# A two-layer graph kernel in float32: x kept on chip, a fourth PSUM bank for second products, and 110 adjacency tiles loaded in pairs

## The reference

```python
# x, u: 8192 x 64;  adj: 8192 x 8192;  weight: 64 x 64;  bias: 64;  all float32
x1 = layernorm(x + adj @ (x * (u >= 0.1) / 0.9))
x2 = layernorm(x1 + adj @ (x1 @ weight) + bias)
```

## Time and profile before

| | |
|---|---|
| median of 3 runs | 898.15 us (898.11 to 898.16) |
| profiled execution | 898.45 us, span 896.5 us, granted clock 0.995 |
| PE busy | 863.1 us, 96% |
| DVE busy | 560.9 us, 63% |
| read from memory | 356.61 MB |
| transfers of 1 MB | 334 |

### The profile page before, as it was taken

One profiled execution on the slowest core, in us unless ns is written; L12 is line 12 of the kernel. 1 busy time (PEld: TensorE's weight loads), 2 busy tenths in 40 slices (PEclk: granted clock), 3 DMA queues, 4 the chain that ended last, 5 costly groups with the idle time before them and its releaser, 6 DMA issues.

```text
span 896.5 us, 15757 instructions
## 1 busy us (share of the span) xinstructions
PE 863.1 (96%) x6790; PEld 482.7 (54%) x6790; DVE 560.9 (63%) x1144; ACT 21.3 (2%) x59; POOL 25.3 (3%) x24
## 2 busy tenths in 40 slices
PE   3899999999999999999999999999999999999996
PEld 2664554445767546555555564646545566456432
DVE  6356123145155757775777777778777777867755
ACT  0100000000000000000000000000000000000011
POOL 3000000000000000000000000000000000000133
PEclk9999999999999999999999999999999999999998
DMA  9999999999999999999999999999999999999962
GB/s 373 412 416 420 421 419 420 421 420 421 420 420 420 419 421 419 421 400 402 420 421 406 423 419 397 419 372 422 372 410 421 415 423 419 420 423 419 420 256 71
DMA packets 55412, 359.73 MB, mean 401 GB/s; under 512 B 6448, under 2 KB 10544, under 8 KB 12592
## 3 DMA queue, kind: packets, MB, share of 16 engines
q1 hardware_dynamic: 55344, 358.74, 96.9%
HBM read 356.61 MB, written 2.10 MB: 400 GB/s over the span
## 4 chain that ended last, share of the span: by engine, by line
PE 85%; DMA 7%; DVE 4%; SPq 2%; issue 2%; ACT 0%; POOLq 0%; POOL 0%; DVEq 0%
PE psum L1033 20%; PE psum L986 19%; PE psum L967 8%; PE psum L1001 8%; PE psum L995 8%; PE psum L1019 6%; DMA tiles<-adj_chunks 5%; PE psum L953 5%; PE psum L974 4%; PE psum L1039 4%; DMA tiles<-adj_t 2%; PE psum L930 1%; SPq L500 1%; DVE layer L654 1%; DVE layer L709 1%
## 5 line engine op out<-in xcount | busy, mean ns | idle before, releaser
L986 PE MATMUL psum<-tiles,stat 128*64 128x256 f32 x1952 | 218.3, 379 | 1.6 <-DMA tiles<-adj_t 1.6
L1033 PE MATMUL psum<-tiles,stat 128*64 128x512 f32 x944 | 210.3, 593 | 0.6 <-issue 0.3
L654 DVE TENSOR_TENSOR layer<-psum,layer 128x512 f32<-128x512 f32 (+1 forms) x143 | 98.7, 690 | 154.6 <-PE psum L1033 58.0
L986 PEld LDWEIGHTS psum<-tiles,stat 128*64 128x64 f32 x1952 | 147.1, 137 | 72.4 <-issue 7.5
L1033 PEld LDWEIGHTS psum<-tiles,stat 128*64 128x64 f32 x944 | 69.2, 137 | 119.8 <-issue 115.8
L690 DVE TENSOR_TENSOR tiles<-tiles 128x512 f32<-128x512 f32 x90 | 62.2, 691 | 53.8 <-PE psum L976 52.2
L1003 PE MATMUL psum<-tiles,stat 128*64 128x256 f32 x360 | 92.6, 380 | 0.0
L969 PE MATMUL psum<-tiles,stat 128*64 128x256 f32 x360 | 92.4, 379 | 0.0
L967 PE MATMUL psum<-tiles,stat 128*64 128x256 f32 x360 | 92.4, 379 | 0.0
L967 PEld LDWEIGHTS psum<-tiles,stat 128*64 128x64 f32 x360 | 49.3, 137 | 37.8 <-issue 16.7
L678 DVE TENSOR_TENSOR tiles<-tiles 128x512 f32<-128x512 f32 x90 | 60.6, 684 | 8.0 <-DMA tiles<-adj_t 8.0
(11 more groups left out here) (100 smaller groups left out, 852.5 us busy)
## 6 DMA issues: line engine op xcount, KB each, us to landing
tiles<-adj_t SPq DMA_DIRECT2D x306, 1024.0 KB, 13.6
tiles<-adj SPq DMA_DIRECT2D x12, 1024.0 KB, 19.2
tiles<-adj_chunks SPq DMA_DIRECT2D x12, 1024.0 KB, 20.4
tiles<-xu SPq DMA_DIRECT2D x4, 1024.0 KB, 8.0
tiles<-adj_parts SPq DMA_DIRECT2D x16, 256.0 KB, 17.6
x_res<-x SPq DMA_DIRECT2D x16, 128.0 KB, 14.4
out<-layer SPq DMA_DIRECT2D x8, 256.0 KB, 2.2
w<-weight SPq DMA_DIRECT2D x4, 16.0 KB, 10.2
```

What stands on the lines that cost most here:

```text
L654: return dve.tensor_tensor(out=to, in0=addend, in1=to, op=ALU.add)
L986: last = pe.matmul(sum_f[i % 2][to, left], stat[:, j * C + c, 0:D], tile[:, c, columns], start=begun.get("f") != i and c == 0, stop=ends a ...
L1033: last = pe.matmul(bank[to, :], stat[:, j * C + c, D:2 * D], tile[:, c], start=c == 0, stop=c == C - 1)
```

## The change

1. **x kept.** ACT copies x out of the staged `xu` into `stat[:, :, D:2D]` at the start (four copies of 128 x 1024), the place where h will stand later. The 16 loads of `x_res` and their waits on SP go. Loads into the last four slots wait for these copies too.
2. **Fourth bank.** `turned` moves to columns 256 to 511 of the two `sum_f` banks, whose sums fill columns 0 to 255, and `ECHO_BANKS` becomes 4. The rows that next use such a bank wait for `turned_read`, where they waited for the copy of the sum. The old use of 3 in `order_of_work` becomes `JOINS_LAST` = 2, so that the last `chunk` and `rest` of column 0 stand one job earlier in row 2.
3. **Pairs.** Tiles that are on chip for fewer than `SHORT` = 4 jobs are loaded two by two where a slot with an even number and its neighbour are both free no later than `LATER` = 1 job after the second-earliest free slot. The host lays such tiles side by side (`adj_twos`), so that a partition's row is 16 KB long, and one transfer of 2 MB brings both and adds to one semaphore. 110 tiles in 55 transfers are loaded so. Single tiles take, of the free slots, the one whose neighbour is busy longest. All counts `freed` are kept in rising order.

```diff
-ECHO_BANKS = 3
+ECHO_BANKS = 4
+JOINS_LAST = 2
+SHORT = 4
+LATER = 1
+TWOS_OF = ("early", "pair", "first", "raw")
...
-            if pieces and (len(filler) == ECHO_BANKS if i > 1 else len(filler) % 2 == 0):
+            if pieces and (len(filler) == JOINS_LAST if i > 1 else len(filler) % 2 == 0):
...
+    def short(n):
+        tile, begin, uses = needs[n]
+        return len(tile) == 2 and uses[-1] - begin < SHORT and tile_jobs[begin][0] != "part"
...
+    n = 0
+    while n < len(needs):
+        in_order = sorted(free)
+        if n + 1 < len(needs) and short(n) and short(n + 1) and (
+                tile_jobs[needs[n][1]][0] in TWOS_OF):
+            freed, slot = min((max(free[s], free[s + 1]), s) for s in range(0, SLOTS - 1, 2))
+            if freed <= min(needs[n][1], max(latest, in_order[1]) + LATER):
+                take(n, slot)
+                take(n + 1, slot + 1)
+                latest = max(latest, freed)
+                freed_of[n] = freed_of[n + 1] = latest
+                beside[n] = n + 1
+                n += 2
+                continue
+        ready = max(latest, in_order[0])
+        slot = -max((latest > 0 and free[s ^ 1] if s ^ 1 < SLOTS else latest, -free[s], -s) for s in range(SLOTS) if free[s] <= ready)[2]
+        latest = freed_of[n] = ready
+        take(n, slot)
+        n += 1
...
-        x_res = sb("x_res", [P, 2, C * D])
...
-        h_bias = [x_res[:, :, :].rearrange("p n (c d) -> p (n c) d", d=D),
-                  halves[:, :].rearrange("p (c d) -> p c d", d=D)]
+        h_bias = [layer1[:, n].rearrange("p (c d) -> p c d", d=D) for n in (1, 2)]
...
-        turned = banks[4]
-        echo = banks[5:8]
+        turned = [bank[:, B // 2:B] for bank in sum_f]
+        echo = banks[4:8]
...
-                if rows_begun == 0 and part == 1 or rows_begun >= 1 and kind in ("first", "fused") and tile[0] == rows_begun:
-                    i = rows_begun
-                    if i >= 2:
-                        sp.wait_ge(turned_read, turns(i - 2))
-                    sp.dma_start(x_res[:, i % 2], x_v[:, i]).then_inc(s_res[i % 2], 16)
-                    rows_begun += 1
-                if new and staged <= slot:
+                tile, both = loaded[0], len(loaded) == 2
+                if new and staged <= slot + both:
                     sp.wait_ge(dropped, XU)
+                    sp.wait_ge(x_kept, XU)
                 if freed:
                     sp.wait_ge(tile_jobs_done, freed)
+                if both:
+                    sp.dma_start(tiles[:, slot:slot + 2], adj_twos[n_twos]).then_inc(s_arrived[slot], 16)
+                    n_twos += 1
+                    continue
...
+            for g in range(XU):
+                act.wait_ge(s_xu[g], 16)
+                act.activation(rows_of_x(g, slice(D, 2 * D)), xu_stage[:, g, :, 0], ACT.Copy).then_inc(x_kept, 1)
...
-                x_rows = x_res[:, i % 2].rearrange("p (c d) -> p c d", c=C)
+                x_rows = stat[:, i * C:(i + 1) * C, D:2 * D]
...
-                            if i <= 2:
-                                pe.wait_ge(half_by_act, turns(i - 2))
-                            pe.wait_ge(half_by_dve, turns(i - 2))
+                            pe.wait_ge(turned_read, turns(i - 2))
```

More of the change, by code:

```diff
@@ L268, in place_tiles, with take @@
                 del on_chip[tile]
[L270 to L277, removed]
+    def short(n):
+        tile, begin, uses = needs[n]
+        return len(tile) == 2 and uses[-1] - begin < SHORT and tile_jobs[begin][0] != "part"
+    free, latest = [0] * SLOTS, 0
+    slot_of, freed_of, beside = {}, {}, {}
+    def take(n, slot):
+        tile, begin, uses = needs[n]
+        assert free[slot] <= begin, "the order of work needs more slots"
+        free[slot] = uses[-1] + 1
         for m in uses:
             slot_of[m, tile] = (slot, n)
+    n = 0
[17 more added lines that the diff above has]
+        n += 1
     loads, place, landed, whole = [], {}, [0] * SLOTS, set()
+    signal, used = {}, set()
     for m, job in enumerate(tile_jobs):
@@ L288, in place_tiles, with tiles_side_by_side, resnorm_graph_layers @@
                 first_load = n not in whole
+                new = slot not in used
+                tiles_loaded = [tile]
                 whole.add(n)
-                loads.append((tile, job[1] if in_parts else None, slot, freed_of[n] if first_load else 0,
-                              landed[slot] == 0, job[0]))
                 landed[slot] += first_load
-            place[job, tile] = (slot, landed[slot])
+                signal[n] = slot, landed[slot]
+                used.add(slot)
+                if n in beside:
+                    whole.add(beside[n])
+                    tiles_loaded.append(needs[beside[n]][0])
+                    new = new or slot + 1 not in used
+                    used.add(slot + 1)
+                    signal[beside[n]] = signal[n]
+                loads.append((tiles_loaded, job[1] if in_parts else None, slot, freed_of[n] if first_load else 0, new, job[0]))
+            place[job, tile] = (slot, *signal[n])
     return loads, place
-def resnorm_graph_layers(nc: bass.Bass, x, xu, adj_t, adj_parts, adj_0, adj_chunks, weight, bias, out):
+def tiles_side_by_side(loads):
+    return [load[0] for load in loads if len(load[0]) == 2]
+def resnorm_graph_layers(nc: bass.Bass, xu, adj_t, adj_twos, adj_parts, adj_0, adj_chunks, weight, bias, out):
     jobs = order_of_work()
@@ L315, in resnorm_graph_layers @@
         latest_freed = max(latest_freed, load[3])
-        freed_for[load[0], load[5]] = latest_freed
+        for tile in load[0]:
+            freed_for[tile] = latest_freed
     first_sums_from, second_sums_from, chain_at = [], [], 0
@@ L474, in _ @@
                 sp.dma_start(tiles[:, staged + g], xu[g]).then_inc(s_xu[g], 16)
-            rows_begun = 0
-            for n, (tile, part, slot, freed, new, kind) in enumerate(loads):
+            n_twos = 0
+            for n, (loaded, part, slot, freed, new, kind) in enumerate(loads):
                 if n == len(loads) // 2:
@@ L882, in arrived @@
             def arrived(job, tile):
-                slot, load = place[job, tile]
-                pe.wait_ge(s_arrived[slot], 16 * load)
+                slot, signal, load = place[job, tile]
+                pe.wait_ge(s_arrived[signal], 16 * load)
                 if tile[0] == 0 and tile[1] < PARTS:
@@ L1054, in _ @@
                     else:
[L1055 removed]
+                        pe.wait_ge(turned_read, turns(NB - 1))
                         pe.wait_ge(combined, 2 * combined_rows(NB - 1))
```

34 lines of the change are left out of this document (17 added, 17 removed).

## The result

The changed kernel takes 901.13 us in the median of 12 runs (899.04 to 904.15), the kernel before 898.18 us (898.05 to 898.56). The ratio is 1.0035, with an interval of 1.0023 to 1.0046: slower, where 892.8 us was forecast. The profiled execution took 901.12 us.

The account below looks back on a forecast made before the run. PE and DMA were taken to bound the kernel in turns, PE alone late on. Savings of 3.35 us up to 447 us plus 2.0 for the fourth bank, together 5.4, gave 892.8 us, range 890.8 to 897.0.

Parts of the forecast that it names:

- Pairs, issue: On SP's load queue, a pair waits 1.7 or 3.4 us for its second slot, hidden by 4.6 us of cover: nothing.
- cover of 4.6 us: Load issued at 394.8 us: 7.1 us from issue to landing, 2.5 its own transfer, leaving 4.6 against a 3.4 us wait.
- Behind 450 us the queue may run dry, but there tiles lie ready.: Tile loads after 450 us: a dry queue costs nothing, as the last tile lies ready 15 us before its job.
- Pairs, lateness: Joint landing delays `first` jobs where DMA sets the pace, such as 324 us: 0.85 us lost, ends 0 and 1.73.
- x kept: Transfer queue: 16 x transfers of 128 KB go, 0.37 us each, saving 2.6 us by 324 us and 3.7 by 447.
- the bank: PE's waits for DVE's joins behind rows 14 and 15 go: 1.5 us at 781.80 and 0.4 at 847.82, sum 2.0.
- the rate: Rows of 16 KB in pair transfers: 2 MB in 4.91 us in place of 4.97, 0.07 us saved a pair.
- long rows run slower: Rival, chance 0.13: 16 KB rows move slower in tile transfers; 905 us at 0.5 us a pair, up to some 980.
- More than this: Rival, chance 0.06: pairs relieve the queue at once, 2 MB landing closer than 2 x 2.49 us; all tile waits go, 887.0.
- The relief is eaten: Rival, chance 0.15: lateness at 324 and 448 us or one dry queue up to 447 us takes 3.35 us; 896.2 or 897.
- behind 324.2 us PE is alone: Chain in order of time: behind the second-stretch DMA end at 324.2 us there is only PE for over 500 us.

Follow-up runs that it names:

- split: Changed kernel with its slots and SP waits kept, but each pair issued as two 1 MB transfers with a semaphore each: 897.51 us.
- x_bank: Changed kernel without pairs, so x kept on chip and the fourth bank only: 892.97 us.
- own_wait: Changed kernel with the planner's pair slots, but no 2 MB transfers: each tile loaded when its own slot is free, the earlier slot first: 894.82 us.
- split_15: Changed kernel with only the pair (15,0) and (1,8) issued as two transfers with a semaphore each: 899.17 us.
- later_4: Changed kernel with LATER = 4 jobs in place of 1, giving 116 pairs: 906.01 us.
- three_banks: Changed kernel with three banks for second products in place of four, pairs kept: 905.55 us.

## Why the prediction was wrong

**The failed step is "Pairs, issue".** I wrote that a pair waits for a second slot at most one job longer than for the second-earliest free slot, 1.7 or 3.4 us, and set this against 4.6 us of cover. The rule says one job behind the *second-earliest* slot. What is lost is counted from the *first* free slot, for which a single tile would have waited. In a run of equal jobs the two slots come free one job apart and the error is small. At a row end they don't. There the row's last four `first` jobs use tiles that stay `held`, and by the plan the second slot came five jobs after the first. SP stood 15.2 us in place of at most 10.0 in one piece, (8,2) was issued 12.3 us later (396.7 against 384.4) and landed 5.0 us later. The cover of 4.6 us that I quoted was read at 394.8 us, 10 us from this very place, and in a kernel in which SP issued a tile in between. In place of "nothing" the wait cost 4.5 us by `split` against `x_bank`, and in the traces it lies in PE's waits at 438.7 and 443.7 us.

**The 4.5 us have two parts.** 2.7 by `own_wait` against `split` are the wait for the pair's second slot. 1.85 by `own_wait` against `x_bank` are a free slot that is passed over, since it isn't one of the pair. At (8,2) both are one wait: five of its six jobs behind count 174 belong to the second part. The edit on the choice of slots stood in the diff, and I gave it no term.

**"Behind 450 us the queue may run dry, but there tiles lie ready."** The evidence was the slack at the very end, 15 us at 866 us. At 593.9 us, when (12,2) landed before, PE was 9 us from its job. The pair was issued 16.3 us later, and PE waited 2.06 us at 607.8, with 0.16 on top. The late issue alone didn't do it: `split` has it too, and no wait. Both tiles had to land first. The slack should have been read at each row end, not at the last.

**"Pairs, lateness"** had the right mechanism and too small a size. I put 0.85 us, with 1.73 as the upper end; joint transfers cost 3.6 us by `split` against the change. Both the places and the kinds of job were too few. At 404 and 607 us the joint landing of a pair of `raw` tiles, issued late, costs 0.95 and 2.06 us that `split` doesn't have. By the plan 23 pairs, and not 16, lie ahead of 324 us. For jobs that use both tiles I took no loss, but the planner also pairs the second tile of one `early` job with a tile of the next, (15,0) with (1,8), and PE stood 3.74 us there, 1.5 more than in `x_bank` and the longest wait for a tile behind the opening. The part of it that lasted wasn't settled by `split_15`.

**Right were** the two parts other than pairs: x kept 3.1 us, the bank 2.1 us against 2.0, with the row at 781.80 as its place and no DVE wait behind rows 14 and 15. Right was the rate too: 2 MB in 4.87 to 4.90 us against 4.91. The rival "long rows run slower" ended on the right side for a wrong reason: the packets are not slower. "More than this" had 2 MB land well within 2 x 2.49 us; `later_4` has 4.87 to 4.90, 0.1 us less a pair, and with the 424 GB/s that refutes it. The Trainium skill (DMA: Bandwidth & Descriptors, Anatomy of one DMA) names a fixed cost of about 2 us a DMA, fitted to transfers that GpSimd issues; here SP issues them, and 55 transfers fewer gave no such time back. "The relief is eaten" came nearest, with a queue that runs dry. It ran dry twice where PE noticed, and my price for it ended at the size of the relief, though nothing ends it there. One reading was wrong without harm: behind 324.2 us PE is alone for 442 us and not for over 500, since from 766.7 to 781.7 us the chain runs mostly through DVE, ahead of the wait at 781.80 that the sum did count.

**The sum in terms measured:** 898.2 - 3.1 (x) - 2.1 (bank) + 1.85 (slots passed over) + 2.7 (wait for the second slot) + 3.6 (joint landing) = 901.15, against 901.13. The terms are differences between neighbouring kernels, so they add up by construction; each one by itself is uncertain by about a microsecond, as most kernels with pairs scatter by 1 to 5 us from run to run, while the kernel before stays within 0.9 and `x_bank` within 0.4. Part of this scatter goes with TensorE's clock: in the changed kernel the six executions up to 901.12 us have a mean granted clock of 0.994 or 0.995, the six above it 0.991 to 0.993. By an estimate, 0.001 of it is 0.9 us in 900. In `split` and in the kernel before the clock moves as much and the time doesn't follow. Why stays open.

## What to carry to other kernels

Where one queue issues in order, price a merged load from the moment at which its first part alone could have gone, and do it at the place where buffers come free farthest apart, not in the steady stretch. A transfer for two buffers takes the landing time of both, and in the full queue of this kernel it gave back only 0.1 us (4.87 to 4.90 against 2 x 2.49). Load a tile as soon as any buffer is free: here keeping x and adding the bank without pairs took 892.97 us, the best version of this study.

## What was unexpected of the hardware

- A long wait of PE cost more than its length at 94 us. The granted clock from 94 to 104 us was 0.83 behind the wait of 3.74 us, and 1.00 in the kernel before, where the wait was 1.03 us. That is 3.4 of 10 us at 1.2 GHz in place of 2.4, and the `early` jobs behind it took 8.78 us, where others of 32 records take 6.87. `x_bank` has 0.83 from 92 to 102 us too, behind a wait of 2.23 us. At 440 and 607 us waits of 1.86 and 2.06 us were followed by 1.00, but in `three_banks` one of 2.03 us at 608.7 by 0.83. So the length of the wait alone doesn't tell. After and then before:

```profile
94.00:104.00 10.00, 9.10 (x38) 3.77 (x40) 0.28 (x1) 0.00 (x0) 0.00 (x0) 0.83 1.01 425
```

```profile
94.00:104.00 10.00, 10.00 (x64) 5.33 (x62) 1.38 (x2) 0.00 (x0) 0.00 (x0) 1.00 1.01 423
```

- ACT's copy of 1,024 columns in float32 took 1.06 us, where I had put 2 as the bound:

```profile
5.78 1.06 ACT L597 ACTIVATE stat<-tiles 128x1024 f32<-128x1024 f32 x1 [3.77 <-DMA tiles<-xu]
```
